# Graph attention in a vision tower: eight picking turns and 32 gathers per row of edges, in place of seven and 36

## The reference

```python
h = (x_flat @ W_gat).reshape(M, HEADS, NUM_EXPERTS)        # M = 8192, 4 heads, 4 values
src = concat([edge_index[0], loops]); dst = concat([edge_index[1], loops])
a_src = (h * att_src).sum(-1); a_dst = (h * att_dst).sum(-1)
e = leaky_relu(a_src[src] + a_dst[dst], negative_slope=0.2)
ee = exp(e - segment_max(e, dst)[dst])
alpha = ee / (segment_sum(ee, dst)[dst] + 1e-16)
agg = segment_sum(h[src] * alpha[:, :, None], dst) + b_gat
scores = layernorm(agg).reshape(M, HEADS, NUM_EXPERTS).mean(1)   # gate of the experts
```

## Time and profile before

| | |
|---|---|
| median of three runs | 10221.51 us (10212.16 to 10259.31) |
| the profiled execution | 10204.01 us, span 10201.9 us |
| TensorE busy, share of the span | 8118.3 us, 80% |
| VectorE busy | 6919.7 us, 68% |
| GpSimd busy | 5470.0 us, 54% |
| ScalarE busy | 4660.6 us, 46% |
| gathers of this stage, GpSimd line 2938 | 1188, 1152.7 us busy |
| matmuls of this stage, line 2955 | 11088, 1327.4 us busy |

### The profile page before, as it was taken

How to read it: one execution, slowest core, us unless ns; L and a number is a source line. 1 busy time by engine, 2 the same in 40 slices (tenths; PEclk the granted TensorE clock), 3 DMA queues, 4 the chain that set the end, 5 groups by cost and what they waited for, 6 DMA issues and landing times. The chain is left out here.

```text
span 10201.9 us, 186539 instructions
## 1 busy us (share of the span) xinstructions
PE 8118.3 (80%) x76884; PEld 4869.9 (48%) x76884; DVE 6919.7 (68%) x10011; ACT 4660.6 (46%) x10721; POOL 5470.0 (54%) x5545
## 2 busy tenths in 40 slices
PE   4999899999999996278788888886667568888847
PEld 2666566666656663122222222223332457777732
DVE  7888878700000378778899999995454568888853
ACT  5344444443444333133577777784333333333322
POOL 0067777777776000074566666676043267777730
PEclk7999899989999997578899999997667689999966
DMA  5010100010010000000000000000000032222210
GB/s 181 22 42 26 37 23 26 23 38 25 23 39 21 31 24 27 10 2 1 3 2 2 2 2 2 2 2 1 1 1 1 14 36 51 44 48 47 44 51 9
DMA packets 274885, 251.29 MB, mean 25 GB/s; under 512 B 204401, under 2 KB 258161, under 8 KB 268340
## 3 DMA queue, kind: packets, MB, share of 16 engines
q1 hardware_dynamic: 96724, 219.26, 6.6%
q0 software_dynamic: 177312, 20.11, 3.4%
HBM read 178.16 MB, written 60.82 MB: 23 GB/s over the span
## 5 line engine op out<-in xcount | busy, mean ns | idle before, releaser
L2498 POOL DMA_INDIRECT sorted<-by_row_rows,r_pos x2112 | 2082.8, 986 | 2502.1 <-ACT e_xt L1354 1422.2
L2652 POOL DMA_INDIRECT sorted<-r_rows,r_pos x2112 | 2087.1, 988 | 1193.0 <-issue 643.2
L2171 DVE TENSOR_TENSOR a_top<-bank,a_k 128x2048 f32<-128x2048 f32 x896 | 1972.5, 2282 | 7.1 <-ACT a_qs L2226 6.9
L2955 PE MATMUL bank<-g_parts,g_hot 128*128 128x256 bf16 x11088 | 1327.4, 286 | 293.9 <-DVE g_hot L2995 159.6
L2955 PEld LDWEIGHTS bank<-g_parts,g_hot 128*128 128x128 bf16 x11088 | 1133.2, 103 | 487.9 <-issue 142.3
L2938 POOL DMA_INDIRECT g_g<-table,g_el x1188 | 1152.7, 970 | 362.2 <-issue 362.2
L2373 PE MATMUL bank<-a_top,sc_pick_row 128*32 128x512 f32 x7168 | 952.3, 615 | 306.3 <-DVE a_top L2171 290.4
L847 DVE TENSOR_TENSOR f_qa<-f_qa,bank 128x512 f32<-128x512 f32 x128 | 82.3, 684 | 1576.9 <-PE bank L624 1340.0
L2613 DVE TENSOR_TENSOR_SCAN r_work<-r_hit,r_base 128x528 f32<-128x528 bf16 (+3 forms) x900 | 1045.9, 1162 | 29.1
L615 PE MATMUL bank<-f_space,f_proj 128*128 128x512 f32 x2048 | 986.5, 609 | 86.2 <-ACT f_space L752 83.8
L2219 ACT ACTIVATE a_over<-a_k,a_qs 128x64 f32<-128x64 f32 x4096 | 1021.2, 336 | 0.0
(11 more groups left out here) (587 smaller groups left out, 11729.7 us busy)
## 6 DMA issues: line engine op xcount, KB each, us to landing
f_wm<-folded SPq DMA_DIRECT2D x16, 4608.0 KB
sorted<-r_rows,r_pos POOLq DMA_INDIRECT x2112
sorted<-by_row_rows,r_pos POOLq DMA_INDIRECT x2112, 2.1
g_near<-near SPq DMA_DIRECT2D x231, 128.0 KB
states<-g_st SPq DMA_DIRECT2D x33, 768.0 KB, 3.8
g_g<-table,g_el POOLq DMA_INDIRECT x1188
fp_raw<-t_modes SPq DMA_DIRECT2D x4, 2304.0 KB, 15.8
folded<-fp_turned SPq DMA_DIRECT2D x16, 576.0 KB, 8.8
```

Source lines behind the costliest of these rows:

```text
L2171: v.tensor_tensor(top[:, n % RD].rearrange("p q (h s) -> p q h s", s=S), q, kk, ALU.max).then_inc(top_done, 1)
L2498: p.indirect_dma_start(out=self.dst, out_offset=bass.IndirectOffsetOnAxis(ap=self.idx[:, k:k + 1], axis=0), in_=self.rows[:, k, :], in_off ...
L2652: p.indirect_dma_start(out=self.dst, out_offset=bass.IndirectOffsetOnAxis(ap=self.pos[:, at:at + 1], axis=0), in_=self.rows[:, part % 2, a ...
L2955: last = pe.matmul(out, hot[:, n % HB, k, j * P:(j + 1) * P], parts[:, k, s].rearrange("p f i -> p (f i)"), start=(k == 0 and s == 0), sto ...
```

## The change

The number of picking turns of a row goes from seven to eight. A turn picks four columns, so `TURNED` goes from 28 to 32 and `ASKED`, the number of gathers in a row, from 36 to 32. All else follows from these numbers: the near parts that are listed and stored in `graph_table` have 32 columns a row, the far mask, the own scores and their buffers are 32 columns wide, and the loops over turns run eight times a row (264 turns in place of 231).

```diff
 NEAR = 4
 FAR = TILES // NEAR
 PICK_COLS = 4
-PICKS = 7
+PICKS = 8
 TURNED = PICKS * PICK_COLS
 ASKED = RUN - TURNED
```

## The result

The changed kernel takes 10414.2 us (median of four runs, 10396.0 to 10427.2), the kernel before 10231.7 us beside it (four runs): ratio 1.0175, 95% interval 1.0144 to 1.0207. It is slower by 182 us, as forecast (184 us; 10405 in the range 10360 to 10443). The kernel before had 10221.5 us in the forecast; a fourth run raised its median by 10 us.

A forecast was written before the change was run, and what follows sets the result against it. The prediction took each row as bound by VectorE's serial stretch, then TensorE's dense turns, with GpSimd hidden. Turn 172.9 + wider operations 11.1 = 184 us on the 10221.5 median gave 10405 us, range 10360 to 10443.

The forecast's parts named there:

- What bounds a row: Graph attention's row loop: 24.7 us of VectorE in series, then 22.8 us of TensorE's turns; both free of GpSimd.
- The eighth turn: End of TensorE's dense stretch: 5.24 us more a row, 172.9 us over 33 rows, all on the path.
- One more load, and the table stage: SyncE's eighth near-row load and the wider table operations and store ahead of the rows: both hidden, costing nothing.
- Wider operations: Own scores and mask in VectorE's serial stretch, 512 columns for 448: 0.34 us a row, 11.1 us in all.
- The gathers: Four fewer gathers a row free 168 us of GpSimd, costed at nothing because no one waits for them.
- The clock: TensorE's slow starts behind dry spells: same share, 28 of 32; bounds 47 us less or 7 us more.
- The sum: Whole kernel: 172.9 + 11.1 = 184 us more, a median of 10405 us, 1.8% slower.
- Gathers as the bound: Rival: GpSimd sets the pace of the rows, so four fewer gathers give back 168 us, 10053 us; 4%.
- The dry spells as cover: Rival: TensorE's idle 7.2 us a row swallows the new turn, leaving 11 us, 10232 us, no change; 5%.

The follow-up runs named there:

- E1: Changed kernel (eight turns) with 36 gathers a row, the four extra landing in a buffer nothing reads: 10377.1 us, ratio 1.0151 to the kernel before.
- E2: Kernel before (seven turns) with only 32 gathers a row from the fourth row on: 10219.2 us, ratio 1.0000 to the kernel before.
- E3: Kernel before with six turns and 40 gathers a row, the same edit the other way: 10341.6 us, ratio 1.0122.
- F1: Changed kernel with 16 of 48 matmuls in the last turn of each row: 10352.5 us, ratio 1.0129 to the kernel before.
- the repeat: The changed kernel itself measured again, unaltered, on another chip: 10386.8 us, ratio 1.0164 to the kernel before.
- F3: Changed kernel (eight turns, 32 gathers) with hot tiles four turns ahead instead of two, rings enlarged: 10100.0 us, ratio 0.9874 to the kernel before.
- F2: Kernel before (seven turns, 36 gathers) with hot tiles four turns ahead instead of two, rings enlarged: 10168.0 us, ratio 0.9945.
- F4: Changed kernel with hot tiles four turns ahead and 36 gathers, four into an unread buffer: 10194.2 us, ratio 0.9964 to the kernel before.

## Why the prediction was right, step by step

*What bounds a row.* Right: VectorE's serial stretch and TensorE's dense one, GpSimd beside both. E1 and E2 show it from both sides, E3 shows where it stops.

*The eighth turn, 5.24 us.* Right: the same spacing in the changed profile, and F1 shows that TensorE's work makes it, down to VectorE's share (predicted 3.26, measured 3.31 us).

*One more load, and the table stage: nothing.* Right. ScalarE waits for near rows as long as before, 296.5 us in 32 waits (shown above) against this line of the kernel before:

```profile
ACT g_apart L2967 <- DMA g_near<-near: 299.1, 32, 10.1
```

From line 2832 in the table stage to TensorE's first matmul of the row loop it is 128.5 us (8136.5 to 8264.95), against 130.4 (8083.6 to 8214.02).

*Wider operations, 0.34 us a row.* Right for the operations: the own scores take 686 to 695 ns instead of 620 to 626 and the mask 684 instead of 619, together 0.33 us a row. But VectorE's serial stretch as a whole, from the start of a row's last products (line 3009) to the hot tile behind the state scans (line 2995), grew by 0.25 us a row: over 32 rows 777.49 - 769.35 = 8.14 us, not 10.9.

*The gathers, nothing.* Right, with the pauses, the line that ends them and the lead of 100 us as forecast.

*The clock.* The term that was off. The sum took the old share of slow starts, 28 of 32. In the changed profile 22 bursts begin slow and 10 don't, as in these rows of TensorE alone:

```profile
8438.06 36.85 PE L2955 MATMUL bank<-g_parts,g_hot 128*128 128x256 bf16 x336 [2.09 <-DVE g_hot L2995]
...
8645.92 38.16 PE L2955 MATMUL bank<-g_parts,g_hot 128*128 128x256 bf16 x336 [3.49 <-DVE g_hot L2995]
```

So 32 spaces grew by 1680.3 - 1517.6 = 162.7 us and not by 32 x 5.58 = 178.6. Of these 16 us 13 lie in TensorE's dense stretch, from the hot tile of line 2995 to the next row's last products: over 32 rows it grew by 902.86 - 748.24 = 154.62 us and not by 32 x 5.24 = 167.7. Six fewer slow starts of 1.67 us are 10 of them, and nine slow ones that lose 1.3 us for 1.67 another 3. The other 3 of the 16 are the serial stretch above. The prediction had set 47 us as the bound for the clock.

*The sum.* 184 us forecast, 168 us by the stage's own rows, 182 us between the medians. That the medians come within 2 us of the forecast is partly luck: the repeat gives 171 us, and executions differ by tens of microseconds in layers ahead.

*The rivals.* Gathers as the bound: false at seven and eight turns with a lead of two, true at six turns and, with 36 gathers, at a lead of four. The dry spells as cover: false at this lead. What shortens them is a longer lead together with fewer gathers (F3), not another turn.

## What to carry to other kernels

Before work is moved from one engine to another, see in the waits whether anyone waits for the engine that is to be relieved: at 97% of the row's length GpSimd was still worth nothing. Where a row is a serial stretch of one engine and a dense stretch of another, work that is added to the dense one costs its full length; how far the one runs ahead over the other's serial stretch is then the number to change first (here 57 us by itself, in F2). After that the bound is elsewhere and the same edit can have the other sign (here +171 us at a lead of two, -68 us at a lead of four).

## What the runs showed of the hardware

Whether TensorE starts fast or slow behind a short idle spell is not settled by the length of the spell alone. In the changed profile the ten bursts that began behind spells of 1.9 to 2.54 us started fast and the 22 behind 2.55 to 4.0 us slow. But the first such burst of the row loop, in the same place and behind the same spell, is fast in the changed profile and slow in its repeat:

```profile
8333.10 36.85 PE L2955 MATMUL bank<-g_parts,g_hot 128*128 128x256 bf16 x336 [1.97 <-DVE g_hot L2995]
```

```profile
8293.37 38.52 PE L2955 MATMUL bank<-g_parts,g_hot 128*128 128x256 bf16 x336 [1.97 <-DVE g_hot L2995]
```

The second spell isn't independent of what stands ahead of it either: it is shorter where the turn before it is slower (2.09 us behind a turn of 8.26, 3.49 behind one of 6.67), and the two mostly add up to 10.1 to 10.4 us. In F4, with one spell a row and no such turn, bursts started fast behind spells of up to 2.88 us and slow behind those of 3.1 us and more.

A row of the changed kernel took about 51.4 us with a fast start and about 53 with a slow one, and rows of a kind came in runs. Of 32 starts 28 were slow in the kernel before and in E2, 22, 20 and 20 in the changed kernel, its repeat and E1, and 30 in F1. So the count looks tied to the kernel more than to the execution, on one to three profiles of each row length. What in the kernel sets it, the length of a row (47.4, 52.5 and 51.0 us) or the spells (the first one is some 6 us in F1), no run here separates. A change that moves a row by a few microseconds can move this term, by up to 32 x 1.67 = 53 us here, and a forecast can only bound it.
